# Attention with experts on one core: the product for the next maxima first in four groups of a turn, and fewer full products

## The reference

```python
xn = layernorm(x)                                   # no scale, no shift
# attention, 16 heads of 8 channels
q, k, v = heads(xn @ wq.T + bq), heads(xn @ wk.T + bk), heads(xn @ wv.T + bv)
scores = einsum('bthd,bshd->bhts', q, k) * 8 ** -0.5
scores = where(xn[:, :, 0] != 0, scores, -inf)      # mask over keys
attn = softmax(scores, axis=-1)
attention = einsum('bhts,bshd->bthd', attn, v).reshape(B, T, C) @ wo.T + bo
# 8 experts, 2 of them for each token, each with room for 1280 tokens
logits = xn @ gate_w; top2; router_probs = softmax over the two
ffn = combine(gelu(rows_of_expert @ c_fc + fc_bias) @ c_proj + proj_bias)
out = x + attention + ffn
```

## Time and profile before

| what | value |
| --- | --- |
| time, median of 3 executions | 589.01 us (587.32 to 593.07) |
| the profiled execution | 585.37 us |
| its span, first to last instruction | 583.3 us |
| PE busy in the span | 541.7 us (93%) |
| DVE busy | 437.4 us (75%) |
| ACT busy | 372.2 us (64%) |
| POOL busy | 202.1 us (35%) |
| mean granted share of PE's clock | 0.995 |

### The profile page before, as it was taken

How to read it: one execution, slowest core, us unless ns; L and a number is a source line. 1 busy time by engine, 2 the same in 40 slices (tenths; PEclk the granted TensorE clock), 3 DMA queues, 4 the chain that set the end, 5 groups by cost and what they waited for, 6 DMA issues and landing times.

```text
span 583.3 us, 11531 instructions
## 1 busy us (share of the span) xinstructions
PE 541.7 (93%) x4404; PEld 304.8 (52%) x4404; DVE 437.4 (75%) x665; ACT 372.2 (64%) x753; POOL 202.1 (35%) x218
## 2 busy tenths in 40 slices
PE   3886999999999999998999999999999999999995
PEld 2552533344443443436999999997434444344343
DVE  4969979989989998996234333313998998999876
ACT  2653077977878778777333444434697787877873
POOL 3887724655555500030011111010455555452000
PEclk9999999999999999999999999999999999999997
DMA  7786273232222212151433443412323223221012
GB/s 190 235 259 190 90 284 109 79 88 66 68 87 75 71 40 51 31 157 46 129 86 94 132 132 93 125 46 61 73 77 83 67 63 87 71 67 51 1 56 91
DMA packets 57766, 56.89 MB, mean 98 GB/s; under 512 B 8816, under 2 KB 44656, under 8 KB 57712
## 3 DMA queue, kind: packets, MB, share of 16 engines
q1 hardware_dynamic: 51920, 42.25, 25.8%
q0 software_dynamic: 5792, 13.90, 7.8%
HBM read 29.91 MB, written 25.69 MB: 95 GB/s over the span
## 4 chain that ended last, share of the span: by engine, by line
PE 74%; DVE 11%; ACT 9%; DMA 3%; issue 1%; SPq 1%; ACTq 0%; DVEq 0%
PE bPV L980 19%; PE bD L937 13%; PE bD L1095 12%; PE bX L960 8%; ACT probs L598 7%; DVE nmax L746 5%; PE bX L1079 3%; PE bX L1081 3%; PE bX L1080 3%; PE bD L989 3%; PE bX L1048 2%; DMA stacks<-hid 2%; PE bPV L1120 2%; PE bD L1001 2%; DVE hid L690 1%
## 5 line engine op out<-in xcount | busy, mean ns | idle before, releaser
L746 DVE TENSOR_REDUCE nmax<-bD 128x2 f32<-128x1024 f32 x256 | 302.6, 1221 | 27.5 <-PE bD L937 24.8
L598 ACT ACTIVATE probs<-bX 128x512 f32<-128x512 f32 x512 | 265.9, 600 | 37.2 <-PE bX L960 37.2
L960 PE MATMUL bX<-QK 32*128 32x512 f32 x512 | 160.5, 492 | 4.5 <-ACT probs L598 3.6
L980 PE MATMUL bPV<-probs,v_aug 128*32 128x256 f32 (+1 forms) x1920 | 160.0, 405 | 0.0
L937 PE MATMUL bD<-QK 30*128 30x512 f32 x512 | 127.0, 494 | 7.0 <-DVE nmax L746 5.9
L937 PEld LDWEIGHTS bD<-QK 30*128 30x128 f32 x512 | 47.4, 181 | 116.0 <-issue 89.1
L629 ACT ACTIVATE hid<-bX,fcb 128x512 f32<-128x512 f32 (+1 forms) x96 | 55.6, 615 | 70.5 <-PE bX L1081 70.2
L960 PEld LDWEIGHTS bX<-QK 32*128 32x128 f32 x512 | 69.8, 181 | 23.2 <-ACT probs L598 8.6
L501 POOL DMA_INDIRECT slot_x<-xn_all,put_i x64 | 62.2, 972 | 53.9 <-DMA slot_x<-xn_all,put_i 38.4
L1095 PE MATMUL bD<-wpj,hid 128*128 128x128 f32 x640 | 72.8, 275 | 0.0
L1095 PEld LDWEIGHTS bD<-wpj,hid 128*128 128x128 f32 x640 | 72.1, 192 | 0.0
(11 more groups left out here) (107 smaller groups left out, 461.5 us busy)
## 6 DMA issues: line engine op xcount, KB each, us to landing
stacks<-hid SPq DMA_DIRECT2D x16, 512.0 KB, 5.0
QK<-stacks SPq DMA_DIRECT2D x128, 64.0 KB
slot_x<-hid POOLq DMA_DIRECT2D x10, 512.0 KB, 3.6
xe<-slot_x SPq DMA_DIRECT2D x8, 640.0 KB, 4.8
slot_y<-ye SPq DMA_DIRECT2D x8, 640.0 KB, 4.3
QK<-stacks SPq DMA_DIRECT2D x128, 36.0 KB
acc<-in_x SPq DMA_DIRECT2D x8, 256.0 KB, 5.0
QK<-nmT SPq DMA_DIRECT2D x128, 4.0 KB
```

Of the source, the lines that this page charges most:

```text
L598: taken(nc.scalar.activation(probs[:, (g % 2) * 4 + i, :], next_x()[:], ACT.Exp, scale=SCALE))
L746: nc.vector.tensor_reduce(nmax[q][:, k, 2 * pair:2 * pair + 2], bank()[:], AX.X, ALU.max, negate=True).then_inc(s_dd, 1)
L960: filled(nc.tensor.matmul(next_x()[:], K[u][q][rows_used, j * P:(j + 1) * P], Q[u][q][rows_used, :], start=True, stop=True))
L980: last = nc.tensor.matmul(bPV[32 * h:32 * h + 32, at], v_aug[b % 2][:, j, u * UH + QUAD * q + h, :], probs[:, (g % 2) * 4 + h, at], start= ...
```

## The change

Three edits, all in the order of work; no product that is used is added or dropped.

1. In the groups for which `early` is true, PE's order is A0 S2 S3 V0 S0 S1 V1 A1 in place of S0 S1 V0 A0 S2 S3 V1 A1, and ACT takes the exponentials in the order of heads 2, 3, 0, 1. These groups are 6 and 10 of every turn, and 2 and 4 of every turn but the first.
2. `maxima` on PE moves from the start of groups 2, 6, 10, 14 to the end of groups 1, 5, 9, 13. It now stands before the full products, the sums and the projection of these places, and not behind them. The order of the `bX` fills is the same, and ACT's and SP's code is unchanged for it.
3. The three full products after group 1 stay in the first turn only. Those after group 9 stay, behind the sums.

```diff
+def early(g, first):
+    return g in (GROUPS + 2, PROJECTED_AT + 1) or (g in (2, TURNED_AT + 1) and not first)
+
+def heads(g, first):
+    return (2, 3, 0, 1) if early(g, first) else (0, 1, 2, 3)
...
@@ ScalarE, group
-                for i in range(QUAD):
-                    if i == 0:
-                        wait(act, s_pv, n - 1)
-                    taken(nc.scalar.activation(probs[:, (g % 2) * 4 + i, :], next_x()[:], ACT.Exp, scale=SCALE))
+                wait(act, s_pv, n - 1)
+                for h in heads(g, b == 0):
+                    taken(nc.scalar.activation(probs[:, (g % 2) * 4 + h, :], next_x()[:], ACT.Exp, scale=SCALE))
...
@@ TensorE, scores
-                if j == 0 and h == 0:
+                if j == 0 and h == heads(g, b == 0)[0]:
                     pe.wait_ge(s_nq[q], (b * UNITS + u) * (MAX_DMAS * 16) + MAX_DMAS * 16)
...
-                if h == QUAD - 1:
+                if h == heads(g, b == 0)[-1]:
                     exp_done[b * GB + g] = x.value()
...
@@ TensorE, group
-                if g % 4 == MAXIMA_AT and not (last and g // 4 == 3):
-                    maxima(b * HALVES + g // 4 + 1, (g // 4 + 1) % 2)
-                scores(b, g, 0)
-                scores(b, g, 1)
-                values(0)
-                ahead(0)
-                scores(b, g, 2)
-                scores(b, g, 3)
-                values(1)
-                ahead(1)
-                if g % GROUPS == 1:
+                def full_products():
+
                     unused = next_x()
                     for _ in range(3):
                         nc.tensor.matmul(unused[:], ones_r[:], hot_f, start=True, stop=True)
+
+                order = heads(g, b == 0)
+                if early(g, b == 0):
+                    ahead(0)
+                    scores(b, g, order[0])
+                    scores(b, g, order[1])
+                    values(0)
+                else:
+                    scores(b, g, order[0])
+                    scores(b, g, order[1])
+                    values(0)
+                    ahead(0)
+                scores(b, g, order[2])
+                scores(b, g, order[3])
+                values(1)
+                ahead(1)
+                if g % 4 == MAXIMA_AT - 1 and not (last and g // 4 == 3):
+                    maxima(b * HALVES + g // 4 + 1, (g // 4 + 1) % 2)
+                if g == 1 and first:
+                    full_products()
                 if g == 1 and not first:
                     output_sums(b - 1, 1)
                 if g == TURNED_AT and not first:
...
                 if g == GROUPS + 1:
                     output_sums(b, 0)
+                    full_products()
```

## The result

The kernel after takes **585.59 us** (median of 20 executions, 583.39 to 594.08) against 587.51 of the kernel before on the same chips, ratio **0.9956, interval 0.9935 to 0.9978**. It is a little faster, 2.6 us by the ratio (1.3 to 3.8 by its interval). The ratio leaves out the executions that are more than 1.5% above the fastest of their kernel (one of the kernel before took 789.6 us), and the medians of all lie 1.9 us apart. I had forecast 590.2, +1.2 us: the sign was wrong. My own range, 587 to 593, doesn't hold the 585.59, nor does the range of 8 in 10, 586 to 594; carried over by the ratio, 589.0 x 0.9956 is 586.4, which only the wider one holds. By 1% the time is the same, which had a chance of 0.81.

A forecast was written before the change was run, and what follows sets the result against it. PE's order of work was taken to bound the kernel. Border terms, mostly small losses against -0.80 in the first turn, summed to +1.2 us, 590.2 from a 589.0 median; range 587 to 593, 8 in 10 586 to 594.

The forecast's parts named there:

- the latency: Groups 2, 6, 10: PE starts A0 0.14 us after DVE's reduce ends, a figure taken from the projection's start.
- the sum: All border terms over the eight turns, first turn included, added to +1.2 us.
- The new waits: Groups 2, 6, 10: A0 waits for DVE's reduce of the previous A1; at group 2, 0.84 us of idle PE.
- my lower bound of 0: Smallest latency allowed between reduce and A0; at 0, 21 borders win 0.14 each, -2.9 us.
- The link of 0.04: Early groups: S to first exponential takes 0.63 us instead of 0.59 when an A starts together with S.
- My bounds: Limits on wait latency, link over 29 groups and PE's fresh start: -2.9 to +3.4 us round the median.
- DVE's head start: Earlier A0 only moves DVE's idle time ahead of A1, worth 0; the rival that it pays had chance 0.06.
- The wait ahead of the projection: Group 5 into 6: PE's 0.70 us wait for A0 of group 5 remains, since A1 of group 4 isn't earlier.
- -0.80: First turn: earlier transpose and DMAs remove the wait of group 4's first S, 0.80 us gained.
- The +0.59: First turn, group 6: A0 first waits for its bank, +0.55 us, and the link adds +0.04.
- The clock: Rival: PE's clock falls in the idle stretch after group 1, giving 599 to 616 us; chance 0.12.
- The freed 0.80: Rival: dropped full products after group 1 show because A0 needn't wait for DVE, giving 584.3 us; chance 0.04.

The follow-up runs named there:

- e_only: Kernel before with only the early order (A0, heads 2 and 3 first) in groups 2, 4, 6, 10; 587.9 us at clock 0.990, ratio 1.0033.
- a_full: Kernel after with the three full products after group 1 put back behind the sums; group 1 to 2 takes 4.585 us against 4.559 to 4.564.
- k_pre: Kernel after with two more full products in groups 1 and 9; group 1 to 2 takes 4.553 us against 4.564.
- m_only: Kernel before with only the transpose of the maxima moved ahead of full products, sums and projection; 582.9 us at clock 0.990.
- f_only: Kernel before without the three full products after group 1 of turns 1 to 7; group 1 to 2 3.946 us against 4.560, median moved by 2 us.
- a_pre: Kernel after without its early order, with two full products added in groups 1 and 9; mean clock 0.991, no time given.
- p_pre: p_mid with two full products added in groups 1 and 9; 574.59 us.
- p_mid2: p_mid run again, unchanged, on another chip; 574.92 us, ratio 0.9788 to the kernel before.
- p_mid: Kernel after without its early order, projection and its transpose moved into group 6 behind S0 and S1; ratio 0.973 to the kernel before, on a slow chip.
- p_mid9: p_mid without the three full products after group 9 as well; median 8 us longer than p_mid on the slow chip.

## Why the prediction was wrong, point by point

The step that turned the sign is the latency, the 0.14 from a reduce's end to A0's start: the runs show 0.06 to 0.10, and 1.5 us of the sum hang on it. Two things more leave the 585.59 outside my range. The sum gave the granted clock no term at all: in the runs it is worth another 0.9 to 2.4 us, and its cause stays open. And the kernel before took 587.51 beside the result, 1.5 less than the 589.0 from which I had started.

- **The new waits were right, their latency mis-sized.** A0 waits for A1's reduce in groups 2, 6 and 10, as the rule of the `bD` banks has it. I took 0.14 from the end of a reduce to PE's start; it is 0.05, 0.07 and 0.09 at the three borders. The projection's own start, from which I had the 0.14, is a different one: 0.15 at every such border, before and after, and no run shows why it is longer. That is half way to my lower bound of 0. With 0.07 the three borders come out at +0.01, -0.07 and +0.01, and 0.00, -0.07 and +0.03 were measured.
- **The link of 0.04** was right: 0.63 from S to exponential in the kernel after (122.79 to 123.42) at every early group, and +0.04 from group 3 to 4. (My bounds count 29 groups with it; there are 30.)
- **DVE's head start pays nothing**: right. It is idle 0.96 before A1 in place of 0.66 before A0.
- **The wait ahead of the projection stays**: right, 1.19 behind A1 against 1.20.
- **The first turn**: -0.80 was forecast for the DMA wait, -1.30 came in this pair, some -0.7 over all profiles. Besides, the transpose's new place gave 0.09 at group 1, which had no term. I had read the 0.85 of idle PE as the whole delay; the S also lost going together with A1, so the border was 1.30 over 2.28. The +0.59 came as +0.51.
- **The sum** with the measured terms is -1.0 in the pair of profiles and -0.4 with the mean DMA wait; at equal clock the executions say -0.4 to -1.0. This is where the sign turned: small terms of both signs, and the one positive term taken from another kind of start at 21 borders (0.14 in place of 0.07, 1.5 us). The +1.2 without these 1.5 is already negative.
- **The clock** had no term in the sum. I had it as a rival that could only make the kernel slower, because the page of the kernel before shows full clock; that was one execution with 0.995, where its mean is 0.981. Against 0.995 the mean clocks of the two kernels cost an estimated 3 us (0.987) and 6 us (0.981), at 0.41 for 0.001. Which part of the change does this, if any, is open: e_only, a_full and k_pre, which share the early order, have 0.986; m_only has 0.982, f_only 0.977; but a_pre, p_pre and p_mid2, without it, have 0.988 to 0.991. By the rule that the prediction took from the Trainium skill ("TensorE: Matmul & The Clock Gate", Part 1 and Part 4, on idle time and transposes) there could have been more falls after the change; the mean clocks, 0.987 after and 0.981 before, don't show that.
- **The freed 0.80** (first rival): right that they don't show behind A0's wait. f_only shows them with S first, as 0.62.

## What to carry to other kernels

A product moved to the front of PE's order brings its bank's wait with it: look up who last used the bank, and when that reader is done. Where such a wait is longer than the work ahead of it, dropping work there gains nothing (0.02 to 0.03 a border here, a_full against the kernel after); take the gain by putting work that needs no such bank first, and by laying the border's work over the wait (p_mid). Before a forecast of a fraction of a per cent, ask how the clock varies between executions, since one profile shows only one draw of it.

## What the runs showed of the hardware

- The mean granted clock of one kernel differs between executions on the same chip, from 0.966 to 1.000 for the kernel before in the second set. Nearly all spread of its times goes with it: 0.41 us for 0.001 in the first set, with 1.2 us left round the line. One chip gave every kernel less (0.945 for the kernel before, 623 us).
- Whether full products behind a border hold the clock is not shown: without those after group 9 it was 0.908 +-0.008 against 0.936 +-0.009 on the chip with the low clocks (p_mid9, p_mid); with and without those after group 1 it was 0.986 and 0.987 (a_full, the kernel after).
- From a DVE reduce's end to a PE product that waits for its bank 0.06 to 0.10 us pass (the kernel after, groups 2, 6 and 10), 0.15 to the projection.
